# How B reaches the state scan: two fp32 transposes, or one bf16 selection matmul on B split in three parts

## The reference

```python
x_dbl = einsum('bld,ed->ble', u, xp_w)            # u: silu of the causal convolution
dt, Bm, C = split(x_dbl, [16, 16 + 64])           # per token
dt = softplus(einsum('blr,dr->bld', dt, dtw) + dtb)
for each token t:
    h = h * exp(dt_t * A) + (dt_t * u_t)[:, None] * B_t[None, :]     # [512, 64]
    y_t = sum over states of h * C_t
```

## Time and profile before

| | us |
|---|---|
| median of 3 runs | 3443.27 |
| lowest and highest of them | 3443.0 and 3447.5 |
| the profiled execution's own time | 3447.5 |
| its span, first to last instruction | 3445.4 |
| DVE busy in the span | 3128.8 (91%) |
| PE busy, granted clock 0.921 | 2658.9 (77%) |
| ACT busy | 2753.4 (80%) |
| POOL busy | 2672.9 (78%) |

### The profile page before, as it was taken

The page is one execution under the profiler, slowest core; times in us unless marked ns, Lnnn a source line. Parts: engine busy times, 40 slices in busy tenths (PEclk is TensorE's granted clock), DMA queues, the critical chain, the costliest instruction groups (busy, mean ns, idle before and its releaser), DMA issues.

```text
span 3445.4 us, 51757 instructions
## 1 busy us (share of the span) xinstructions
PE 2658.9 (77%) x18080; PEld 2299.5 (67%) x18080; DVE 3128.8 (91%) x2270; ACT 2753.4 (80%) x6338; POOL 2672.9 (78%) x1299
## 2 busy tenths in 40 slices
PE   5767676777767788878787688878877778888776
PEld 4666565666656677767676677767766667777665
DVE  4999999999999999999999999999999999999600
ACT  6879888897989789797988679888887879877322
POOL 5889888887989788787888778787897778877401
PEclk7899999998999899999999899999998889999888
DMA  2241111111111134314231143423321132334376
GB/s 91 81 143 62 50 47 44 57 49 47 53 47 45 53 108 136 117 64 134 90 103 54 49 132 115 140 83 96 113 74 56 41 120 84 123 121 140 98 258 188
DMA packets 151735, 319.15 MB, mean 93 GB/s; under 512 B 28570, under 2 KB 44963, under 8 KB 151092
## 3 DMA queue, kind: packets, MB, share of 16 engines
q1 hardware_dynamic: 147522, 305.08, 27.3%
q0 software_dynamic: 3072, 8.39, 0.7%
q10 hardware_dynamic: 882, 2.38, 0.2%
HBM read 285.90 MB, written 29.88 MB: 92 GB/s over the span
## 4 chain that ended last, share of the span: by engine, by line
issue 34%; DVE 32%; PE 13%; POOL 11%; ACT 9%; DMA 1%; SPq 0%; POOLq 0%; DVEq 0%; ACTq 0%
DVE h L1114 15%; DVE psX L1104 14%; POOL hC L892 9%; ACT dA L1082 3%; PE psY L1377 3%; PE psG L1328 3%; PE psX L1361 2%; ACT xs L1057 2%; PE psX L1328 2%; PE psG L1405 1%; PE psX L1405 1%; POOL dtu L834 1%; POOL dt L829 1%; DVE gT L1128 1%; ACT gT L941 0%
## 5 line engine op out<-in xcount | busy, mean ns | idle before, releaser
L892 POOL TENSOR_TENSOR hC<-h,cb 128x1024 f32<-128x1024 f32 x1024 | 2406.7, 2368 | 541.4 <-DVE h L1114 533.3
L1114 DVE TENSOR_TENSOR_SCAN h<-dA,psX 128x1024 f32<-128x1024 f32 (+1 forms) x1114 | 2311.1, 2104 | 57.1 <-PE psX L1361 32.9
L1082 ACT ACTIVATE dA<-dt,negA 128x255 f32<-128x255 f32 x4096 | 1719.5, 502 | 169.7 <-DVE h L1114 165.5
L1377 PE MATMUL psY<-ident,hC 128*128 128x128 f32 x8192 | 1155.8, 288 | 52.3 <-DVE gT L1128 41.3
L1377 PEld LDWEIGHTS psY<-ident,hC 128*128 128x128 f32 x8192 | 1011.6, 150 | 67.3 <-DVE gT L1128 44.9
L1104 DVE TENSOR_TENSOR psX<-dtu,psX 128x1024 f32<-128x1024 f32 x588 | 710.2, 1208 | 51.6 <-POOL dtu L834 35.7
L1361 PE MATMUL psX<-ident,xs 128*128 128x128 f32 x3488 | 522.9, 299 | 273.8 <-DVE h L1114 167.0
L1361 PEld LDWEIGHTS psX<-ident,xs 128*128 128x128 f32 x3488 | 429.6, 153 | 370.5 <-issue 194.4
L1057 ACT ACTIVATE xs<-dtuT,bT 128x512 f32<-128x512 f32 x872 | 579.8, 717 | 10.9 <-PE psX L1361 10.6
L1352 PE MATMUL psX<-ident,bT 128*128 128x128 f32 x1176 | 254.3, 300 | 266.6 <-DVE h L1114 265.2
L1352 PEld LDWEIGHTS psX<-ident,bT 128*128 128x128 f32 x1176 | 134.9, 143 | 390.2 <-DVE h L1114 370.3
(11 more groups left out here) (208 smaller groups left out, 1798.7 us busy)
## 6 DMA issues: line engine op xcount, KB each, us to landing
cb<-c_dram SPq DMA_DIRECT2D x256, 512.0 KB, 3.7
w_up<-in_w_exp SPq DMA_DIRECT2D x201, 256.0 KB, 2.9
w_down<-in_w_exp SPq DMA_DIRECT2D x201, 256.0 KB, 2.8
dA<-in_w_exp SPq DMA_DIRECT2D x39, 256.0 KB, 4.0
h<-in_w_exp SPq DMA_DIRECT2D x39, 256.0 KB, 4.6
x_slots<-got SPq DMA_DIRECT2D x16, 512.0 KB, 5.4
xg<-x_slots SPq DMA_DIRECT2D x60, 128.0 KB, 2.9
y_slots<-yg SPq DMA_DIRECT2D x60, 128.0 KB, 3.0
```

Of the source, the lines that this page charges most:

```text
L892: eng.tensor_tensor(hC[i % NHC][:, :, :], h[i % NH][:, :, :], cw.to_broadcast([P, KI, L]), ALU.mult).then_inc(times_c, 1)
L1082: made = eng.activation(dA[j % NA][:, c, 1:L], dt[n % 2][:, c, 1:L], ACT.Exp, scale=negA[:, JOBS[n][0], c, s:s + 1])
L1114: made = eng.tensor_tensor_scan(h[i % NH][:, part, :].rearrange("p c t -> p (c t)"), dA[i % NA][:, part, :].rearrange("p c t -> p (c t)"), ...
L1377: made = eng.matmul(psY[:, tc, c * P:(c + 1) * P], hC[i % NHC][:, c, tc * P:(tc + 1) * P], ident[:, :], start=s == 0 and c == 0, stop=Fals ...
```

## The change

B is no longer brought to the plain steps by transposes of `bT`. Instead:

- The B products now put states on the partitions: the weights `w_x` hold the 32 low states three times over, then the 32 high states three times over, and `b` makes two outputs of 96 partitions x 256 tokens (four pieces of two products, where there were two pieces of four products with 64 columns).
- ACT copies the result twice (`b_hi`): rounded to bf16 into `bparts` and in fp32 into `b32`. POOL subtracts (`b_rest`), ACT rounds the rest to bf16 (`b_mid`), POOL subtracts again (`b_rest2`), and ACT writes the second and third bf16 part into partitions 32 to 95 of `bparts` (`b_lo`, two copies). `b_rest` and `b_rest2` use a piece of `gT`, so `gate` gets a wait for `b_lo`.
- `spread_b` is one bf16 matmul: the stationary operand is a column of `sel` (three stacked 32x32 unit matrices, 96 rows) broadcast to 128 columns, the moving one is `bparts`, 96 x 256. It adds the three parts up.
- The turned steps still need `bT`: eight small transposes of `b32` (`b_turn`), then `bT_copy` as before. Both are planned in `tasks_turned`, and for job 0 that is beside the first steps of the loop.
- `w_x` is loaded whole by one DMA instead of in three cuts, 272 columns instead of 144. POOL's set-up gets a memset and three selects for `sel`.

```diff
 # tasks_pre
-            task("b", n, 0, "PE", 8 * TURN, ("silu", n, 0), opens="G"),
-            task("b+", n, 0, "PE", 8 * TURN, ("b", n, 0)),
-            task("bT_copy", n, 0, "ACT", 330, ("b+", n, 0), frees=("b", n, 0))]
+            task("b", n, 0, "PE", 2 * MM, ("silu", n, 0), opens="G"),
+            task("b+", n, 0, "PE", 2 * MM, ("b", n, 0)),
+            task("b", n, 1, "PE", 2 * MM, ("b+", n, 0)),
+            task("b+", n, 1, "PE", 2 * MM, ("b", n, 1)),
+            task("b_hi", n, 0, "ACT", 2 * EVICT, ("b+", n, 1), *((("b_rest", n - 1, 0),) if n else ()), frees=("b", n, 0)),
+            task("b_rest", n, 0, "POOL", 1200, ("b_hi", n, 0)),
+            task("b_mid", n, 0, "ACT", EVICT, ("b_rest", n, 0)),
+            task("b_rest2", n, 0, "POOL", 1200, ("b_mid", n, 0)),
+            task("b_lo", n, 0, "ACT", 2 * EVICT, ("b_rest2", n, 0))]
 # tasks_turned
+    out = [task("b_turn", n, 0, "PE", 4 * TURN, ("b_hi", n, 0), opens="G"),
+            task("bT_copy", n, 0, "ACT", 330, ("b_turn", n, 0), frees=("b_turn", n, 0))]
 # SP
-            for to, at, many in ((0, 0, HALF), (HALF, 3 * HALF, HALF), (S, 6 * HALF, S + R)):
-                eng.dma_start(w_x[:, :, :, to:to + many], io["w_x"][:, :, :, at:at + many]).then_inc(mamba_in, 16)
+            eng.dma_start(w_x[:, :, :, :], io["w_x"]).then_inc(mamba_in, 16)
 # POOL
+                    elif name == "b_rest":
+                        k, at = turn["b", n, 0]
+                        on.wait_ge(free[k], at + 1)
+                        on.wait_ge(tap_added, (n + 1) * 2 * (TAPS - 1))
+                        eng.tensor_tensor(brest, b32[:, :, :], bparts[n % 2][:, :, :], ALU.subtract).then_inc(b_rest_done, 1)
+                    elif name == "b_rest2":
+                        on.wait_ge(b_rest_done, n + 1)
+                        on.wait_ge(b_mid_done, n + 1)
+                        eng.tensor_tensor(brest, brest, bmid[:, :, :], ALU.subtract).then_inc(b_rest2_done, 1)
 # ACT
+                    elif name == "b_hi":
...
+                        eng.activation(bparts[n % 2][:, :, :], two(k)[0:3 * HALF, :, :], ACT.Copy).then_inc(b_hi_done, 1)
+                        eng.activation(b32[:, :, :], two(k)[0:3 * HALF, :, :], ACT.Copy).then_inc(free[k], 1)
+                    elif name == "b_mid":
...
+                        eng.activation(bmid[:, :, :], brest, ACT.Copy).then_inc(b_mid_done, 1)
+                    elif name == "b_lo":
...
+                        eng.activation(bparts[n % 2][mid, :, :], bmid[mid, :, :], ACT.Copy)
+                        eng.activation(bparts[n % 2][low, :, :], brest[low, :, :], ACT.Copy).then_inc(b_lo_done, 1)
 # DVE, gate
+                    on.wait_ge(b_lo_done, n + 2)
 # PE, spread_b
-                evicted(("b", n, 0))
+                on.wait_ge(b_lo_done, n + 1)
                 on.wait_ge(scanned, i - 1)
-                for tc in range(KL):
-                    made = eng.transpose(psX[i % 2][:, KI - 1, tc * P:(tc + 1) * P], bT[n % 2][:, tc, s:s + 1].to_broadcast([P, P]), ident[:, :])
-                made.then_inc(x_in, 1)
+                eng.matmul(psX[i % 2][:, KI - 1, :], sel[:, s % HALF:s % HALF + 1].to_broadcast([3 * HALF, P]), bparts[n % 2][:, s // HALF, :],
+                           start=True, stop=True).then_inc(x_in, 1)
 # PE, small work
-                        made = product(dst[:, i * S:(i + 1) * S], [(u[n % 2][:, c, i * P:(i + 1) * P], w_x[:, l, c, 0:S]) for c in range(KI)])
+                        made = product(dst[0:3 * HALF, part * L:(part + 1) * L],
+                                       [(w_x[:, l, c, part * 3 * HALF:(part + 1) * 3 * HALF], u[n % 2][:, c, :])
+                                        for c in (2 * i, 2 * i + 1)], not second, second)
+                    elif name == "b_turn":
+                        k, dst = open_bank((name, n, part))
+                        evicted(("b", n, 0))
+                        for tc in range(KL):
+                            for half in range(2):
+                                at = tc * S + half * HALF
+                                made = eng.transpose(dst[:, at:at + HALF], b32[0:HALF, half, tc * P:(tc + 1) * P], ident[0:HALF, 0:HALF])
+                        made.then_inc(full[k], 1)
```

More of the change, by code:

```diff
@@ L148, in tasks_turned @@
                 task("dtu_copy", n, tc, "ACT", EVICT, ("dtu_turn", n, tc), frees=("dtu_turn", n, tc))]
-    out.append(task("skip", n, 0, "ACT", 4 * HALF_EVICT, ("dtu", n, 1), ("c_copy", n, 0), ("bT_copy", n, 0)))
+    out.append(task("skip", n, 0, "ACT", 4 * HALF_EVICT, ("dtu", n, 1), ("c_copy", n, 0), ("b_hi", n, 0)))
     return out
@@ L480, in decoder_block @@
         w_in = sb("w_in", [P, LAYERS, KD, 2 * DI])
-        w_x = sb("w_x", [P, LAYERS, KI, 2 * S + R])
+        w_x = sb("w_x", [P, LAYERS, KI, 6 * HALF + S + R])
         shared = sb("shared", [P, LAYERS * DI])
@@ L508, in decoder_block @@
         bT = [sb(f"bT{i}", [P, KL, S]) for i in range(2)]
+        b32 = sb("b32", [3 * HALF, 2, L])
         cdt = sb("cdt", [P, L])
+        bparts = [sb(f"bparts{i}", [3 * HALF, 2, L], BF16) for i in range(2)]
+        bmid = sb("bmid", [3 * HALF, 2, L], BF16)
         dA = [sb(f"dA{i}", [P, KI, L]) for i in range(NA)]
@@ L606, in decoder_block @@
         tapped_by, tap_added, silued = sem("tapped_by"), sem("tap_added"), sem("silued")
-        dt_ended = sem("dt_ended")
+        b_hi_done, b_mid_done, b_rest2_done, b_lo_done = sem("b_hi"), sem("b_mid"), sem("b_rest2"), sem("b_lo")
+        b_rest_done, dt_ended = sem("b_rest_done"), sem("dt_ended")
         skipped, logged, dtu_done = sem("skipped"), sem("logged"), sem("dtu_done")
@@ L863, in _ @@
                                        pattern=[[-1, P]], channel_multiplier=1))
+            on.wait_ge(set_up, own.value)
+            own.mark(eng.memset(sel[:, :], 0.0))
+            for part in range(3):
+                on.wait_ge(set_up, own.value)
+                own.mark(eng.affine_select(out=sel[:, :], in_=sel[:, :], compare_op=ALU.not_equal, fill=1.0,
+                                           base=-HALF * part, pattern=[[-1, HALF]], channel_multiplier=1))
             for tile, value in ((ones_row[:, :], 1.0), (neg_half[:, :], -0.5), (cdt[DT0:DT0 + 32, :], 1.0)):
@@ L971, in small_work @@
                     elif name == "bT_copy":
-                        k, at = turn["b", n, 0]
+                        k, at = turn["b_turn", n, 0]
                         on.wait_ge(full[k], at + 1)
-                        on.wait_ge(x_in, S * (n - 1))
                         eng.activation(bT[n % 2][:, :, :], bank[k][:, 0:KL * S].rearrange("p (a s) -> p a s", a=KL),
@@ L1448, in small_work @@
                             k, dst = open_bank((name, n, part))
-                            on.wait_ge(mamba_in, 16 * 5)
+                            on.wait_ge(mamba_in, 48)
                             on.wait_ge(silued, n + 1)
-                        made = product(dst[0:S + R, 0:L], [(w_x[:, l, c, S:2 * S + R], u[n % 2][:, c, :])
+                        made = product(dst[0:S + R, 0:L], [(w_x[:, l, c, 6 * HALF:6 * HALF + S + R], u[n % 2][:, c, :])
                                                            for c in (2 * i, 2 * i + 1)], not second, second)
```

23 lines of the change are left out of this document (18 added, 5 removed).

## The result

The changed kernel takes 3467.9 us (median of four, 3465.1 to 3469.7), the kernel before 3445.1 us beside it. The ratio is 1.0067 (95% interval 1.0052 to 1.0082): 0.7% slower, 23 us. The forecast was 3448.4 us with a range up to 3463: too low by 19.5 us. The profiled execution has a span of 3466.5 us, 21.1 more than before, and took 3468.3.

The account below looks back on a forecast made before the run. DVE was taken to bound the loop. Head +3.5, ACT +4.6 and spreads -3 gave +5.1 us: 3452.6 for the profiled execution, 3448.4 us for the median, which is 4.2 lower; range 3436 to 3463.

Parts of the forecast that it names:

- What bounds the kernel: Whole kernel: DVE bounds the loop, busy 97.4% from 50 to 3200 us, but not the head and tail.
- Spread, -3 us: Plain steps: one bf16 matmul at 0.2 us replaces two transposes at 0.43; DVE gets 3 us back, bounds 0 and 8.
- B products, 0: PE in the loop: wider products add 2.6 us a job, shorter spreads offset them; no net change.
- Head, +3.5 us: Chain before DVE's first step: B products +2.0, b_hi +0.2, b_rest2 +1.3 us; between 1.6 and 7.7.
- ACT and POOL in the loop, +4.6 us: Preparations: ACT's new copies cost DVE 0.8 us in each of six, POOL's pieces nothing; between 0 and 46 us.
- It only rearranges, 0: Whole plan, a rival: pieces placed anew scatter some 5 us either way, widening the forecast; no separate chance given.
- Tail, 0: After the loop: the tail has none of the changed work, so no change.
- ACT becomes the bound: Loop preparations: new ACT time comes out on DVE, up to 46 us; at half, 3467 us; chance 0.22.
- The slow clock: PE in the loop: less work lowers its clock, waits for turned steps double, +33 us, 3477 us; chance 0.07.
- PE's relief: Loop: 120 us less PE work removes half of DVE's 48.3 us of waits on PE, 3427 us; chance 0.19.
- a first step near 44 us: Head: DVE's first step at 44 us, not near 47.0, would mean the B chain is hidden there.
- Named waits above 75 us: Loop: DVE's named waits above 75 us would mean the prediction is wrong, through ACT or the clock.

Follow-up runs that it names:

- e2_after_plan: The kernel before's work (fp32 transposes for the spread, no split) in the changed kernel's written order; 3432.5 us, ratio 0.9962 to the kernel before.
- e3_no_split: The changed kernel in its written order, without the instructions of b_rest, b_mid, b_rest2 and b_lo; 3434.0 us, ratio 0.9966 to the kernel before.
- e4_old_spread: The changed kernel with the spread again by two fp32 transposes of bT, bf16 parts made but unused, in another order; 3469.6 us, ratio 1.0068.
- e12_dtu_later: The kernel before, its planner putting dtu_turn and skip at least 3 us behind dtu's planned end; 3441.6 us, ratio 0.9988.
- e11_plan_dtu_later: The kernel before's work in the changed kernel's order, dtu_turn and skip planned at least 3 us behind dtu's planned end; 3432.4 us, ratio 0.9965.
- e7_hop: The kernel before with the planner's HOP at 110 for 100 ns, the same work in another order; 3449.2 us, ratio 1.0015.
- e8_phantom: The kernel before, its planner charging 1.86 us of ACT a preparation for a piece without instruction, behind bT_copy; 3448.2 us, ratio 1.0005.
- e13_mid_no_wait: The changed kernel with its order and every instruction, but b_mid copies b32 and so does not wait for b_rest; 3443.2 us, ratio 0.9998.

## Why the prediction was wrong, point by point

- **What bounds the kernel**: right. The loop is DVE's, and the loss is DVE standing still in it, 51.3 us of named waits before and 72.2 after.
- **Spread, -3 us**: too large, with little consequence. The bf16 matmul of 256 columns occupied PE for 160.0 / 546 = 0.293 us, not 0.2, so it saves 0.14 us a step. In one order (`e2_after_plan` against `e3_no_split`) DVE's waits for spreads fell from 9.6 to 7.6 us, but those for turned steps rose from 24.5 to 30.0; `e4_old_spread` is 0.01% from the changed kernel, good to some 5 us.
- **B products, 0**: right. 56.1 / 224 = 0.250 us an instruction (0.288 taken), and `e3_no_split`, which has them, is as fast as `e2_after_plan`, which has not.
- **Head, +3.5 us**: it was +0.6, from two parts. The chain was nearly as predicted in this pair of profiles: from the first C product (29.50 us before, 27.33 after) to DVE's first step it grew from 14.0 to 16.75 us, by 2.7. The dt products came 1.75 us later in it (2.0 taken), `b_hi` stands ahead of `soft`, and `b_rest2` between `dt_end` and `dtu` on POOL (39.05). But everything ahead of it was 2.2 us early, of it 2.1 since `w_in` had landed by 11.32 us and not by 13.38. That is the scatter of one execution: in the twelve profiles with the new load of `w_x` the first matmul started at 11.2 to 13.5 us, in the six with the old one at 12.5 to 13.5. The chain's growth is no firmer. With the old work it took 14.0 us in the kernel before, 13.9 in `e12_dtu_later` and 15.0 in `e11_plan_dtu_later`, but 16.6 in `e2_after_plan`, `e7_hop` and `e8_phantom`, where PE's granted clock was 0.50 over its first 9 us (0.73 in the kernel before); the changed chain took about 16.75 us in four profiles. So against these six the change adds anything from 0.1 to 2.9 us there, and PE's clock decides as much as the work does.
- **ACT and POOL in the loop, +4.6 us**: this is the step of the prediction that failed. It priced ACT's new *busy* time, 3.06 us a preparation, and found cover for it; the copies did measure 0.59 and 0.63 us. It looked at POOL's pieces only as delaying `hC`. It never priced the wait of `b_mid` for `b_rest`, although the change's text has it: ACT waits in order for an engine on which a 2.4 us product stands ahead. That wait is 1.95 us a preparation (29.2 / 15), about as much again as the splitting copies, and on top of them it costs 24 us (`e13_mid_no_wait`). The busy time alone costs 11 us, against 4.6 predicted and 46 as its upper bound. I also placed the loss in jobs 0 to 5, where half of the steps are turned. Against `e13_mid_no_wait`, which has the same order, the wait's part gathers all along: counted from each one's first step (44.08 and 46.33 us), the changed kernel's `gate` comes 13.1 us later after job 6 (at 1403.1 against 1392.2 us) and 25.9 us later after job 15 (3253.0 against 3229.4).
- **It only rearranges, 0**: wrong by 13 us in one direction. The changed order with the old work is 0.38% faster than the order before, more than twice what moving HOP did.
- **Tail, 0**: it was -4.4 us, 217.6 for 222.0. It came with the order and not with the work: with the old work in the changed order (`e2_after_plan`) the tail took 215.3 us, and other orders of the old work gave 216.0 to 229.6.
- **The rivals**: "ACT becomes the bound" gave 3467 us, nearly the measured number, by another mechanism: half of 46 us of busy time. The nearness is luck: the busy time is worth 11 us. The slow clock came (0.921 to 0.907), and DVE's waits for turned steps rose by 9 us, not by the 33 of that rival; what part of them is the clock's is open. PE's relief did not come: its spreads took 254.3 us before and 172.8 after, but the B products took 32 us more (32.2 and 64.4), and at the lower clock the transposes of the sums and of the turned steps took 45 us more (1155.8 and 1186.4, 522.9 and 537.5).
- **The signs**: a first step near 44 us was to mean that the B chain is hidden in the head. It came at 44.08, and the chain was not hidden. Named waits above 75 us were to mean ACT or the clock; at 72.2 they just missed that.

The sum that the runs give, against the kernel before: -13 (order, `e2_after_plan`) + 1 (wide products and spread, `e3_no_split`) + 11 (splitting work, `e13_mid_no_wait`) + 24 (the wait on top of it) = +23 us.

## What to carry to other kernels

Price an added piece by its wait as well as by its length: on an engine that executes in order, a piece that needs another engine's result costs the time until that engine gets to it, with everything behind it. Here taking that one wait away gave back 24 of 35 us, where the busy shares had looked harmless on both engines. Test such a wait by pointing the instruction at data that is ready, with the order fixed; shifting it in the planner changes everything else too. With the order fixed, two traces can also be laid side by side step by step, which tells a wait that costs something from one beside which the time is lost anyway. And when a change feeds a planner, time the new order with the old work: it can hide a gain, here 13 us, under the loss.

## What the runs showed of the hardware that was not expected

- The load of `w_in`, 0.5 MB behind which the head waits, had landed anywhere from 11.2 to 13.5 us in the twelve profiles of kernels that issue the loads alike: the start of DVE's work in one profile is good to 2 us at best.
- PE's clock in the head differed between profiles of like work: the eight C products took 2.91 us in the kernel before and 3.67 in `e7_hop`, and with the clock at 0.50 for 9 us the chain behind them grew from 14.0 to 16.6 us.
- Lateness and the low clock came together. Beside job 6, PE stood idle 2.16 us for ACT, and from 1332 to 1338 us its granted clock was 0.50; in the same steps of `e13_mid_no_wait` it was 1.00.
- A single bf16 matmul of 96 x 256 occupied PE 0.293 us here, only a third less than the two fp32 transposes of 128 x 128 that it replaced (0.43 us).
- An ACT copy of 512 elements a partition took 0.58 to 0.59 us from PSUM (96 partitions, to bf16 or fp32) and 0.61 to 0.64 us from SBUF: 32 partitions took as long as 96.
